# The first state of the later pairs: written by ScalarE instead of by bf16 identity products

## The chip, the cores and the metric

One core of a Trainium2 chip. The metric is the device time of one execution in microseconds (us), lower is better. TensorE (PE) does the products, VectorE (DVE), ScalarE (ACT) and GpSimd (POOL) the rest, and SyncE (SP) starts the DMAs. PSUM has eight banks of 128 partitions x 512 floats.

## The reference, cut to what matters

Two layers over a batch of 8 sequences of 512 tokens, 128 wide. Layer 0 is a random-feature attention, a feed-forward block and an expert block. Layer 1 is a "test-time training" layer and then a mixing block. The part of layer 1 that matters here, for each sequence and each of 16 heads (head size 64), over 8 chunks of 64 tokens:

```python
W, b = W1, b1                       # the same first state for every sequence
for chunk in range(8):
    Z1 = xk @ W + b                 # prediction with the old state
    grad = ...                      # a normalisation and its gradient
    W, b = W - (eta * xk).T @ grad, b - sum(eta * grad)
    Zq = xq @ W + b                 # prediction with the new state
    out = xq + gamma * norm(Zq) + beta
```

Every sequence begins with the same state W1, b1. The kernel holds b1 as the 65th row of W1, so the state of one head is 65 x 64.

## The kernel before, in words

The batch is worked through as four pairs of sequences. Layer 0 of pair p+1 is interleaved by hand with layer 1 of pair p: ORDERS (line 104) has one string per engine, each letter one step. A first string is layer 0 of pair 1 alone, a middle string is used for pairs 1 to 3, a last string is layer 1 of pair 4 alone. Every engine goes through its string in order, so the order on each engine is fixed and only semaphores couple the engines. `0` and `1` are steps of layer 0 for the two sequences, `r` the start of a pair, `s` its first state (two steps, one for each half of 8 heads), `k`, `l` the keys and their transpose, `a` the prediction with the old state, `z`, `b`, `c` the gradient, `d` the update of the state, `q`, `e` the queries and the prediction with the new state, `v`, `w` square roots, `f` and `o` the output, `m` the mixing block. A pair has 16 slots of the letters k to f: 8 chunks x 2 halves of heads.

The running state stays in PSUM: banks 0 and 1 hold the first 8 heads of the two sequences, banks 2 and 3 the other 8 heads. `d` on PE (line 607) adds 32 small products onto them with `start=False`. After each `d` ACT copies two banks (65 x 1024 floats) to w_sb in SBUF (`state`, line 780), which `a` and `e` on PE read (line 546). The semaphore w_ready counts these copies.

The first state of a pair is put into the banks by `start_state` on PE (line 557, products on line 564): three bf16 pieces of the state (w_parts, made by POOL in the setup, lines 1296 and 1298) are multiplied by a bf16 identity and added up, which gives the float value. That is 3 products of 65 x 512 for each of two banks, 6 for a step `s`, 12 for a pair. For pairs 2 to 4 PE first waits for w_ready (ACT's last copy out of the banks). The last product raises w_started. ACT waits for it and makes its usual copy to w_sb.

The order around the start of pairs 2 and 3 is, from the middle string:

```python
"PE":  r k s k l s 1 a 0 0 q 1 l b 0 ...
"ACT": r 0 k s k l 1 s m a 0 v 1 q l ...
"DVE": r 0 m 1 0 1 m a z b c a 0 ...
```

and for pair 4, from the last string, `r k s k l s a b b l q a` on PE and `r m k s l a v k s l a v` on ACT.

Other lines that the steps name: L574, the 16 narrow products of `r` (columns of 16) for the learning rate, on DVE L1133 takes them; L590 `k`, L808 its copy on ACT; L539 `l`, L787 and L788 its two copies on ACT (keys); L815 the square after `a` on ACT, L1099 its sum on DVE; L848 the square root of the mixing block's normalisation on ACT, L1151 and L1153 the DVE steps that use it; L1316 the first step of the gradient on POOL. The setup on POOL (lines 1230 to 1303) counts its steps in pool_set; other engines wait for the total N_POOL_SET before layer 1.

Of the kernel before, what the change touches and what calls it, by code (L numbers as in the profile page):

```python
# [1 line left out]

# [8 lines left out]
ACT = mybir.ActivationFunctionType  # L27
# [3 lines left out]
PAIRS = B // 2  # L31
# [8 lines left out]
H, HD, K = 16, 64, 64  # L40
# [3 lines left out]
HH = H // 2  # L44
HALF = HH * HD
C = HD + 1
# [30 lines left out]
def shape_constants():  # L77
# [21 lines left out]
SLOTS = 2 * NJ  # L99
# [2 lines left out]


ORDERS = {
    "PE": (("011011100011000111011011001010110010110100100010"),
        ("rkskls1a00q1lb0nakqn0kbld1aedl1eabk1bqd0lkfqfaed0lqea1kbqlob0d1fk0eafqbnodnlk111ae1fb1kq1dl0aed10lbfk0aed0qbo0"
          "lfk0q1aedb1lqfkaedo0qbl0fma0kbfd0elokqeam10kl0dfqb0ealq10bd1n01faemdob1qf1dfee01offmo1m"),
        ("rksklsabblqakbldkqaekldbqammedlqkfaefbldokamqedblfkaeqbldmafkbledqkofaelbdqmfakqdebqloakkblfdefalobqdkbaeldqfk"
          "eaqlkdfbeamoqldfebqfaeoqdfbmfemodefmfmommmmm")),
    "ACT": (("110110010100110100111101010100010111100100001010"),  # L110
        ("r0kskl1sna0v1ql0a0kvqnkld1aev1lwdeka1wvq0ldfkqafnedlvqawekvqlw1od0fk10eaf1v1qodnlk1wae1vf0kd11lwa0qev0lkdfwa10"
          "veqowdl0fk1aqevd100lfqwkave0qdol0awfvkm0fdel0kowqamve0kl1dfqwe001alv0dq11mfaew0ndvwo1fq1dfewew0off1mom1"),
        ("rmkslavkslavkqldqakevwldkqamvewldkfqaefvdloaqvwkdelmfkewaqvldwmfkamvelqkdwofavledqfakvwdeqlwoaqvkldkffealvwdko"
          "qavelwdqkfeaqvlwdfkmeaolvwfdeqqwfaewovqfdfemowdmefwmfmommmmm")),
    "DVE": (("110110010100101010111101010100010111100010110000"),
        ("r0n101nazbca0z0bc1aezy1beaczy1bc0a0nze1yaebczy0b1aczb101ecyaez111b1cy0az01e0bcyaz0be01c0ayzbcena0zybcmaey0z10m"
          "0ebca0zye101b0yam1czbc0e011eayzbyc0m1eeyny11m"),
        ("rmmazbaczbcazeybcazeybcazebcamyzebcmayzebcayzebcayzebcamzyebcayzbcazebcyazebcyazemybceamyzebcaeyyzbceymmeymmmm"
          "mm")),
    "POOL": ((""),  # L120
        ("zzzzyyzyzyzooyzyzyzyzzoyoyzozyzyyzyyyooo"),
        ("zzzyzyzyzyzyzoyzzyyzozoyzoyzyyzoyyzyyooo")),
}
BANKS = ("01234567023541670237023541670416273501462735014627350146273501462735014627530146275346754675465764756454756475"
          "76745675475647567467467457456745764564576746746576476456746574657465465475645647654765476574657465746574765745"
# [14 lines left out]

def turns(engine):

    first, middle, last = ORDERS[engine]
    taken = dict.fromkeys(PER_TOKEN, 0)
    for what in first + middle.replace("n", "") + (PAIRS - 2) * middle.replace("n", "m") + last:
        pair, step = divmod(taken[what], PER_TOKEN[what])
        taken[what] += 1
        if pair < PAIRS:
            yield what, pair, step
    assert all(n in (0, PAIRS * PER_TOKEN[what]) for what, n in taken.items()), taken  # L150


# [9 lines left out]
def build(nc, a, out):  # L162
    with ExitStack() as ctx:
        def sb(name, shape, dtype=F32):
            return ctx.enter_context(nc.sbuf_tensor(name, shape, dtype))

        def new_sem(name):
            return ctx.enter_context(nc.semaphore(name))


        ps = ctx.enter_context(nc.psum_tensor("ps", [128, 8, 512], F32))
# [5 lines left out]
        def part(pack, name):  # L177
            at, width = views(PACKS[pack])[0][name]
            return tile[pack][:, at:at + width]
# [8 lines left out]
        w_ga, w_i, lora_b, first = (part("expert", n) for n in ("gate_a", "wi", "lora_b", "first"))  # L188
# [14 lines left out]
        ones_bf = sb("ones_bf", [2 * 32 + 1, 128], BF16)  # L203

        w_parts = sb("w_parts", [C, 3, H, HD], BF16)
        ident_bf = sb("ident_bf", [128, 128], BF16)

        mod_all = sb("mod_all", [128, 12, B])
# [31 lines left out]
        w_sb = w_sb_t[0:C]  # L240
# [36 lines left out]
        s_w0 = k_sc[0:C, :, 0:HD]  # L277
# [12 lines left out]
        S = {n: new_sem(n) for n in names}  # L290
# [3 lines left out]
        pool_set, dve_set, act_set, pe_set = (new_sem(n) for n in ("pool_set", "dve_set", "act_set", "pe_set"))  # L294
# [15 lines left out]
        def loaded(eng, name):  # L310

            eng.wait_ge(loaded_sem[name], 16 * len(loads[name]))

        LEVELS = HD.bit_length() - 1
        N_LAYER0_SET = 6
        N_POOL_SET = N_LAYER0_SET + 4 * 4 + 4 + 1 + 1 + 2 * (4 + 1 + 4) + 1 + 4 + LEVELS + LEVELS + 1 + 4 + 5 * 4 + 4 + 8

        x_dram = a["x"].rearrange("b t p d -> b p t d")
        out_dram = out.rearrange("b (j t) d -> b t j d", t=K)
# [15 lines left out]
        def _(pe):  # L335
            count = [0] * 8
            mm = nc.tensor.matmul
# [16 lines left out]
            def end(ins, b):  # L354
                ins.then_inc(S[f"filled_{b}"], 1)
# [9 lines left out]
            for n in range(12):  # L365
                last = mm(bank[7][:, n * B:(n + 1) * B], s_wmod[:, n * D:(n + 1) * D], s_sig[:, n // 6, :], start=True, stop=True)
# [187 lines left out]
                              start=True, stop=True)  # L554
                end(last, b)

            def start_state(p, f):
                for n in (2 * f, 2 * f + 1):
                    if p:
                        pe.wait_ge(S["w_ready"], (SLOTS + 2) * p - 1 + f)  # L560
                    elif count[n]:
                        pe.wait_ge(S[f"drained_{n}"], count[n])
                    for part in range(3):
                        last = mm(bank[n][0:C, :], ident_bf[0:C, 0:C],
                                  w_parts[:, part, HH * f:HH * (f + 1), :].rearrange("c h d -> c (h d)"),
                                  start=(part == 0), stop=(part == 2), skip_group_check=True)
                last.then_inc(S["w_started"], 1)
# [66 lines left out]
            def mixing(p, step):  # L634
# [18 lines left out]
                elif step == MIX_OUT:  # L653
# [3 lines left out]
                        last = mm(bank[b][:, t * D:(t + 1) * D], kact[:, t * 128:(t + 1) * 128], w_vf[:, :], start=True, stop=True)  # L657
                    end(last, b)

            for what, p, step in turns("PE"):  # L660
                if what in "01":
                    layer0(p, step, int(what))
                elif what == "r":
                    if p == 0:
                        loaded(pe, "ttt")
                        pe.wait_ge(pool_set, N_POOL_SET)
                    start(p)
                elif what == "s":
                    start_state(p, step)
                elif what == "o":  # L670
                    attended(p, step)
                elif what == "m":
                    mixing(p, step)
                else:
                    slot(what, p, step)
# [18 lines left out]
        def _(act):  # L694
            loaded(act, "mod")
            nc.scalar.activation(s_sig[:, :, :], cT, ACT.Sigmoid).then_inc(act_set, 1)
            def root(name, src, dst, u=None, scale=1.0, eps=LN_EPS):

                key = name if u is None else f"{name}_{u}"
                nc.scalar.activation(dst, src, ACT.Sqrt, bias=eps, scale=scale).then_inc(S[key], 1)  # L700
# [13 lines left out]
            def layer0(p, step, u):  # L714
# [51 lines left out]
                elif step == LN5:  # L766
                    if p == 0:
                        act.wait_ge(pool_set, N_POOL_SET)
                    elif p >= 2:
# [4 lines left out]
                if step in roots and (p or step != LN1_STATS):  # L774
                    name = roots[step]
                    act.wait_ge(S[f"{name}_var_{u}"], p + 1)
                    root(f"{name}_std", l["mv"][:, :, 1], l["std"][:, :], u)

            def state(f):
                nc.scalar.copy(w_sb[:, f, :, :, :].rearrange("p b h d -> p (b h d)"),  # L780
                               ps[0:C, 2 * f:2 * f + 2, :].rearrange("p a c -> p (a c)")).then_inc(S["w_ready"], 1)
# [84 lines left out]
            for what, p, step in turns("ACT"):  # L866
                if what in "01":
                    layer0(p, step, int(what))
                elif what == "r":
                    start(p)  # L870
                elif what == "s":
                    act.wait_ge(S["w_started"], 2 * p + step + 1)
                    state(step)
                elif what == "o":
                    attended(p, step)
                elif what == "m":
                    mixing(p, step)
                else:
                    slot(what, p, step)
# [3 lines left out]
        def _(dve):  # L883
# [245 lines left out]
            def start(p):  # L1129
                if p == 0:  # L1130
                    dve.wait_ge(pool_set, N_POOL_SET)
                src = filled(dve, f"rate_{p}")[:, 0:NJ * H].rearrange("p (j h) -> p j h", j=NJ)
# [101 lines left out]
        def _(pool):  # L1234
            P = nc.gpsimd
# [18 lines left out]
            def then_all(instructions):  # L1254

                for ins in instructions:
                    done[0] += 1
                    ins.then_inc(pool_set, 1)
                pool.wait_ge(pool_set, done[0])
# [32 lines left out]
            then(P.tensor_scalar(s_mean[:, :], s_mean[:, :], 1.0 / HD, None, ALU.mult))  # L1292
            heads4 = [slice(4 * n, 4 * n + 4) for n in range(4)]
            then_all(tt(s_w0[:, n, :], s_w0[:, n, :], s_mean[:, n].unsqueeze(2).broadcast_to([C, 4, HD]), ALU.subtract) for n in heads4)
            for part in range(3):
                then_all(P.tensor_copy(w_parts[:, part, n, :], s_w0[:, n, :]) for n in heads4)
                if part < 2:
                    then_all(tt(s_w0[:, n, :], s_w0[:, n, :], w_parts[:, part, n, :], ALU.subtract) for n in heads4)
# [3 lines left out]
            then_all(P.memset(t[HD:C, 4 * n:4 * n + 4, :], 1.0) for t in (kT1, qT1) for n in range(4))  # L1302
            assert done[0] == N_POOL_SET, done
            def heads(ap):
# [84 lines left out]
```

## Time and profile before

| | |
|---|---|
| time, median of 3 runs | 1005.95 us (1004.88 to 1006.24) |
| profiled execution, span from first to last instruction | 1004.5 us |
| profiled execution, own time besides the span | not recorded; the span is 1.45 us under the median |
| PE busy, weight loads busy | 94%, 71% of the span |
| DVE, ACT, POOL busy | 78%, 65%, 34% |
| mean granted TensorE clock | 0.977 of full |

Times in rows are in us from the start of the span, durations in us unless "ns" stands there. L12 is line 12 of the kernel before. PE is the row of products, PEld the loads of the stationary operand. In a granted clock 1.00 is 2.4 GHz and 0.50 is 1.2 GHz; a stretch between these was partly at each.

### The profile page before, as it was taken

How to read it: one execution, taken by the hardware profiler on the slowest of the kernel's cores; microseconds unless marked ns; L12 is line 12 of the kernel's file. 1: busy time of each engine (PE TensorE's matmuls, PEld its weight loads, DVE VectorE, ACT ScalarE, POOL GpSimd, SP SyncE). 2: the span in 40 equal slices, each digit the busy share in tenths (PEclk: the TensorE clock that was granted, in tenths of full speed). 3: DMA queues.
4: the chain of work that ended last, by engine and by line, in shares of the span. 5: the costliest groups of instructions: out<-in, count | busy, mean ns of one | idle time of the engine just before them, and what ended most of it. 6: DMA issues, size and time to landing. Idle time of an engine off the chain costs nothing.

```text
span 1004.5 us, 26971 instructions
## 1 busy us (share of the span) xinstructions
PE 949.1 (94%) x10906; PEld 714.9 (71%) x10906; DVE 787.3 (78%) x1945; ACT 651.5 (65%) x1240; POOL 343.0 (34%) x456
## 2 busy tenths in 40 slices
PE   7788899999999999999999999899999998999995
PEld 5565575778787766787887776677787775777773
DVE  5856359988799679968888769987889847888973
ACT  2642274897856575888666566689765556686762
POOL 1992011343341321333242222143341323454450
PEclk9799999999999999979999989999999989999998
DMA  9000010000000010000000010000000000000000
GB/s 333 14 1 1 11 33 1 2 2 2 3 1 3 22 32 1 3 1 3 2 13 1 12 43 2 2 2 2 2 12 2 12 23 2 2 2 13 2 2 21
DMA packets 15831, 16.14 MB, mean 16 GB/s; under 512 B 2013, under 2 KB 14301, under 8 KB 15325
## 3 DMA queue, kind: packets, MB, share of 16 engines
q1 hardware_dynamic: 15709, 14.43, 4.7%
q8 instruction: 87, 1.43, 0.6%
q14 instruction: 35, 0.29, 0.1%
HBM read 10.23 MB, written 2.10 MB: 12 GB/s over the span
## 4 chain that ended last, share of the span: by engine, by line
PE 62%; DVE 24%; ACT 6%; issue 4%; POOL 3%; DMA 0%; DVEq 0%; ACTq 0%; POOLq 0%; SPq 0%
PE ps L546 8%; PE ps L607 4%; PE ps L539 4%; PE ps L631 4%; PE ps L590 3%; PE ps L601 3%; PE ps L528 3%; PE ps L490 3%; PE ps L613 3%; PE ps L520 3%; PE ps L521 3%; PE ps L499 2%; POOL gbase L1316 2%; DVE kmax L1004 2%; DVE tmp L1110 2%
## 5 line engine op out<-in xcount | busy, mean ns | idle before, releaser
L1316 POOL TENSOR_TENSOR gbase<-zhat,gamma 128x512 f32<-128x512 f32 x64 | 81.2, 1269 | 395.1 <-DVE scl L1104 388.5
L1324 POOL TENSOR_TENSOR zq_sqq<-zq_sqq,qinv 128x512 f32<-128x512 f32 x64 | 68.1, 1069 | 185.1 <-DVE qinv L1127 185.1
L780 ACT COPY w_sb<-ps 65x1024 f32<-65x1024 f32 x72 | 72.6, 1008 | 15.6 <-PE ps L607 12.1
L546 PEld LDWEIGHTS ps<-w_sb,keys 65*64 65x64 f32 x2048 | 66.0, 139 | 18.6 <-issue 10.9
L546 PE MATMUL ps<-w_sb,keys 65*64 65x64 f32 x2048 | 73.8, 226 | 3.8 <-ACT zT L835 1.5
L607 PE MATMUL ps<-grad,k_sc 64*65 64x64 f32 x2048 | 74.4, 222 | 2.6 <-DVE grad L1121 2.3
L607 PEld LDWEIGHTS ps<-grad,k_sc 64*65 64x65 f32 x2048 | 66.0, 135 | 14.8 <-issue 12.5
L1107 DVE TENSOR_TENSOR gbase<-gbase,ps 128x512 f32<-128x512 f32 x64 | 43.6, 681 | 40.7 <-POOL gbase L1316 29.3
L546 PEld LDWEIGHTS ps<-w_sb,queries 65*64 65x64 f32 x2048 | 66.2, 140 | 11.5 <-issue 5.4
L613 PEld LDWEIGHTS ps<-h,pack_ttt 128*128 128x128 f32 x512 | 64.5, 194 | 12.8 <-issue 6.6
L546 PE MATMUL ps<-w_sb,queries 65*64 65x64 f32 x2048 | 73.1, 226 | 0.3 <-ACT queries L788 0.2
L590 PE MATMUL ps<-pack_ttt,h 128*128 128x512 f32 x128 | 71.0, 639 | 0.2
L613 PE MATMUL ps<-h,pack_ttt 128*128 128x128 f32 x512 | 69.4, 279 | 1.3 <-ACT keys L788 0.7
L1319 POOL TENSOR_TENSOR k_sc<-k_tok,scl 128x512 f32<-128x512 f32 x64 | 67.8, 1059 | 0.0
L760 ACT ACTIVATE feats<-ps,pack_cols 128x512 f32<-128x512 f32 x64 | 42.9, 687 | 35.3 <-PE ps L521 28.8
L601 PE MATMUL ps<-w_t,h 128*128 128x512 f32 x128 | 65.4, 592 | 0.0
L808 ACT COPY k_tok<-ps 128x512 f32<-128x512 f32 x64 | 37.4, 585 | 42.9 <-PE ps L590 32.7
L631 PE MATMUL ps<-g_wo,zT 128*128 128x128 f32 x512 | 62.4, 275 | 0.0
L631 PEld LDWEIGHTS ps<-g_wo,zT 128*128 128x128 f32 x512 | 59.7, 192 | 0.0
L1099 DVE TENSOR_REDUCE ssum<-sq 128x8 f32<-128x512 f32 x64 | 42.8, 669 | 15.6 <-ACT sq L815 15.6
L815 ACT ACTIVATE sq<-ps 128x512 f32<-128x512 f32 x64 | 38.4, 599 | 22.7 <-PE ps L546 22.1
L1110 DVE TENSOR_TENSOR tmp<-gbase,zhat 128x512 f32<-128x512 f32 x64 | 49.2, 768 | 2.2
(247 smaller groups left out, 2370.9 us busy)
## 6 DMA issues: line engine op xcount, KB each, us to landing
x<-in_x SPq DMA_DIRECT2D x8, 256.0 KB, 3.4
xc<-x SPq DMA_DIRECT2D x16, 128.0 KB, 2.4
out_x<-xc SPq DMA_DIRECT2D x16, 128.0 KB, 2.4
pack_ttt<-in_ttt SPq DMA_DIRECT2D x1, 1216.0 KB
keys<-in_gam_bet_rows SPq DMA_DIRECT2D x1, 1024.0 KB
w_sb<-in_compose SPq DMA_DIRECT2D x1, 1024.0 KB, 10.5
pack_expert<-in_expert SPq DMA_DIRECT2D x1, 792.0 KB, 16.8
zq_sqq<-in_wmod SPq DMA_DIRECT2D x1, 768.0 KB, 4.5
```

Of the source, the lines that this page charges most:

```text
L546: last = mm(bank[b][64 * c:64 * c + 64, (h % HH) * HD:(h % HH + 1) * HD], src[:, h, 64 * c:64 * c + 64], w_sb[:, f, c, h % HH, :], start=T ...
L590: end(mm(bank[b], chunk(p, j), w_k1[:, cols], start=True, stop=True), b)
L601: end(mm(bank[b], chunk(p, j), w_t1[:, cols], start=False, stop=True), b)
L607: last = mm(bank[2 * f + c][0:C, h * HD:(h + 1) * HD], k_sc[64 * c:64 * c + 64, HH * f + h, :], grad[64 * c:64 * c + 64, h, :], start=Fals ...
L613: last = mm(bank[b][:, n * 128:(n + 1) * 128], w_q1[:, (4 * f + n) * 128:(4 * f + n + 1) * 128], chunk(p, j), start=True, stop=True)
L631: last = mm(bank[b][:, 0:D], zT[:, g, :], g_wo[:, g, :], start=False, stop=(g == HP - 1))
L780: nc.scalar.copy(w_sb[:, f, :, :, :].rearrange("p b h d -> p (b h d)"), ps[0:C, 2 * f:2 * f + 2, :].rearrange("p a c -> p (a c)")).then_in ...
L1107: V.tensor_tensor(gbase[:, cols], gbase[:, cols], filled(dve, f"t1_{g}"), ALU.add).then_inc(drained(f"t1_{g}"), 1)
L1110: half_way[0] = go_on(V.tensor_tensor(tmp[:, :], gbase[:, cols], zhat[:, cols], ALU.mult))
L1316: P.tensor_tensor(gbase[:, cols], zhat[:, cols], gamma2[:, cols], ALU.mult).then_inc(S["g_hat"], 1)
L1319: P.tensor_tensor(k_sc[:, hs, 0:HD], heads(k_tok[:, cols]), per_head(scl[:, hs]), ALU.mult)
L1324: P.tensor_tensor(heads(zq_hat[:, cols]), heads(zq_hat[:, cols]), per_head(qinv[:, hs]), ALU.mult).then_inc(S["zq_ready"], 1)
```

## The change

For pair 1 nothing changes. For pairs 2 to 4 the step `s` does nothing on PE. On ACT it waits until the last update of those banks in the pair before is done, and then writes twice from w_first, a float copy of the first state that POOL makes in the setup with four more copies: into the two PSUM banks, and into w_sb. The orders are written out for all four pairs, with the same letters in the same places on every engine. The wait for the end of the setup on PE stands before the first letter of layer 1, which is `r` of pair 1 as before.

```diff
 def turns(engine):
-    first, middle, last = ORDERS[engine]
     taken = dict.fromkeys(PER_TOKEN, 0)
-    for what in first + middle.replace("n", "") + (PAIRS - 2) * middle.replace("n", "m") + last:
+    for what in ORDERS[engine]:
         pair, step = divmod(taken[what], PER_TOKEN[what])
         taken[what] += 1
-        if pair < PAIRS:
-            yield what, pair, step
+        yield what, pair, step
...
         w_parts = sb("w_parts", [C, 3, H, HD], BF16)
+        w_first = sb("w_first", [C, 2, HH, HD])
...
-        N_POOL_SET = N_LAYER0_SET + ... + 1 + 4 + 5 * 4 + 4 + 8
+        N_POOL_SET = N_LAYER0_SET + ... + 1 + 4 + 4 + 5 * 4 + 4 + 8
...
-            def start_state(p, f):
+            def start_state(f):
                 for n in (2 * f, 2 * f + 1):
-                    if p:
-                        pe.wait_ge(S["w_ready"], (SLOTS + 2) * p - 1 + f)
-                    elif count[n]:
+                    if count[n]:
                         pe.wait_ge(S[f"drained_{n}"], count[n])
                     for part in range(3):
                         last = mm(...)
...
                 elif what == "s":
-                    start_state(p, step)
+                    if p == 0:
+                        start_state(step)
...
+            def state0(f):
+                first = w_first[:, f, :, :].rearrange("p h d -> p (h d)").unsqueeze(1).broadcast_to([C, 2, HALF])
+                nc.scalar.copy(ps[0:C, 2 * f:2 * f + 2, :], first)
+                nc.scalar.copy(w_sb[:, f, :, :, :].rearrange("p b h d -> p b (h d)"), first).then_inc(S["w_ready"], 1)
+
...
                 elif what == "s":
-                    act.wait_ge(S["w_started"], 2 * p + step + 1)
-                    state(step)
+                    if p == 0:
+                        act.wait_ge(S["w_started"], step + 1)
+                        state(step)
+                    else:
+                        act.wait_ge(S["dw_done"], SLOTS * p - 1 + step)
+                        state0(step)
...
             then_all(tt(s_w0[:, n, :], s_w0[:, n, :], s_mean[:, n].unsqueeze(2).broadcast_to([C, 4, HD]), ALU.subtract) for n in heads4)
+            then_all(P.tensor_copy(w_first[:, n // 2, 4 * (n % 2):4 * (n % 2) + 4, :], s_w0[:, heads4[n], :]) for n in range(4))
             for part in range(3):
```

## Rows read from the trace of the kernel before

**Rows 1.** The page: the chain that ended last, by engine.
```profile
PE 62%; DVE 24%; ACT 6%; issue 4%; POOL 3%; DMA 0%; DVEq 0%; ACTq 0%; POOLq 0%; SPq 0%
```

**Rows 2.** Groups (mean ns): ACT's state copy; L564: min/median/max ns, first and last start.
```profile
L780 ACT COPY w_sb<-ps 65x1024 f32<-65x1024 f32 x72 | 72.6, 1008 | 15.6 <-PE ps L607 12.1 <-PE ps L564 2.8
...
L564 PE MATMUL ps<-w_parts,ident_bf x48: 377/380/634, 134.3 to 827.9; 65*65 65x512 bf16 x48
```

**Rows 3.** The longest wait of PE between 364 and 590 us (us, times, longest).
```profile
PE ps L412 <- ACT ek L730: 1.5, 2, 0.7
```

**Rows 4.** Timeline, start of pair 2 (start, us, engine, line).
```profile
357.11 1.46 PE L564 MATMUL ps<-w_parts,ident_bf 65*65 65x512 bf16 x6
...
358.51 0.57 ACT L808 COPY k_tok<-ps 128x512 f32<-128x512 f32 x1
358.97 1.01 ACT L780 COPY w_sb<-ps 65x1024 f32<-65x1024 f32 x1
...
359.88 0.59 ACT L808 COPY k_tok<-ps 128x512 f32<-128x512 f32 x1
...
360.95 0.58 ACT L788 COPY keys<-ps 64x512 f32<-64x512 f32 x1
...
361.66 1.01 ACT L780 COPY w_sb<-ps 65x1024 f32<-65x1024 f32 x1
361.68 1.15 PE L546 MATMUL ps<-w_sb,keys 65*64 65x64 f32 x32 [0.51 <-ACT keys L788]
...
362.57 0.20 ACT L848 ACTIVATE std<-mv 128x4 f32<-128x4 f32 x1
...
363.28 1.11 DVE L1153 TENSOR_SCALAR hat<-xc,mv,inv 128x128 f32<-128x128 f32 x4
```

**Rows 5.** Timeline, start of pair 3.
```profile
585.89 1.93 PE L574 MATMUL ps<-w_theta,h 128*128 128x16 f32 x16
...
589.50 2.77 PE L564 MATMUL ps<-w_parts,ident_bf 65*65 65x512 bf16 x6
...
590.42 0.57 ACT L808 COPY k_tok<-ps 128x512 f32<-128x512 f32 x1
...
592.31 1.01 ACT L780 COPY w_sb<-ps 65x1024 f32<-65x1024 f32 x1 [1.32 <-PE ps L564]
...
596.44 1.15 PE L546 MATMUL ps<-w_sb,keys 65*64 65x64 f32 x32
...
597.46 0.20 ACT L848 ACTIVATE std<-mv 128x4 f32<-128x4 f32 x1
...
597.90 1.12 DVE L1153 TENSOR_SCALAR hat<-xc,mv,inv 128x128 f32<-128x128 f32 x4
```

**Rows 6.** Timeline, start of pair 4.
```profile
822.23 0.57 ACT L808 COPY k_tok<-ps 128x512 f32<-128x512 f32 x1
...
823.83 1.01 ACT L780 COPY w_sb<-ps 65x1024 f32<-65x1024 f32 x1 [1.03 <-PE ps L564]
...
828.25 1.15 PE L546 MATMUL ps<-w_sb,keys 65*64 65x64 f32 x32
...
831.38 1.01 ACT L780 COPY w_sb<-ps 65x1024 f32<-65x1024 f32 x1
```

**Rows 7.** Windows: length, busy time of PE, PEld, DVE, ACT, POOL, then granted clock, DMA.
```profile
356.10:366.33 10.23, 9.72 (x82) 6.43 (x79) 9.23 (x46) 8.77 (x17) 0.00 (x0) 1.00 0.11 28
588.01:600.97 12.96, 12.96 (x82) 7.80 (x79) 9.42 (x46) 9.05 (x17) 0.00 (x1) 0.74 0.08 21
426.46:444.96 18.50, 18.50 (x192) 15.50 (x192) 12.81 (x24) 14.50 (x26) 6.20 (x7) 0.72 0.00 1
661.11:676.76 15.65, 15.38 (x192) 12.45 (x192) 12.29 (x23) 14.22 (x26) 5.67 (x7) 0.89 0.01 3
```

**Rows 8.** Timeline of POOL: its setup.
```profile
72.74 1.42 POOL L1296 CAST w_parts<-k_sc 65x256 bf16<-65x256 f32 x4
...
78.53 1.92 POOL L1302 MEMSET queries<- 1x512 f32 x4
```

More of the change, by code:

```diff
@@ L104 @@
 ORDERS = {
[L105 to L122, printed above, removed]
+    "PE": ("011011100011000111011011001010110010110100100010rkskls1a00q1lb0akq0kbld1aedl1eabk1bqd0lkfqfaed0lqea1kbqlob0d1fk0eafqbodlk111ae1fb1kq1dl0aed10lbfk0aed0qbo0lfk0q1aedb1lqfkaedo0qbl0fma0kbfd0elokqeam10kl0dfqb0ealq10bd101faemdob1qf1dfee01offmo1mrkskls1a00q1lb0makqm0kbld1aedl1eabk1bqd0lkfqfaed0lqea1kbqlob0d1fk0eafqbmodmlk111ae1fb1kq1dl0aed10lbfk0aed0qbo0lfk0q1aedb1lqfkaedo0qbl0fma0kbfd0elokqeam10kl0dfqb0ealq10bd1m01faemdob1qf1dfee01offmo1mrkskls1a00q1lb0makqm0kbld1aedl1eabk1bqd0lkfqfaed0lqea1kbqlob0d1fk0eafqbmodmlk111ae1fb1kq1dl0aed10lbfk0aed0qbo0lfk0q1aedb1lqfkaedo0qbl0fma0kbfd0elokqeam10kl0dfqb0ealq10bd1m01faemdob1qf1dfee01offmo1mrksklsabblqakbldkqaekldbqammedlqkfaefbldokamqedblfkaeqbldmafkbledqkofaelbdqmfakqdebqloakkblfdefalobqdkbaeldqfkeaqlkdfbeamoqldfebqfaeoqdfbmfemodefmfmommmmm"),
@@ new lines @@
+    "ACT": ("110110010100110100111101010100010111100100001010r0kskl1sa0v1ql0a0kvqkld1aev1lwdeka1wvq0ldfkqafedlvqawekvqlw1od0fk10eaf1v1qodlk1wae1vf0kd11lwa0qev0lkdfwa10veqowdl0fk1aqevd100lfqwkave0qdol0awfvkm0fdel0kowqamve0kl1dfqwe001alv0dq11mfaew0dvwo1fq1dfewew0off1mom1r0kskl1sma0v1ql0a0kvqmkld1aev1lwdeka1wvq0ldfkqafmedlvqawekvqlw1od0fk10eaf1v1qodmlk1wae1vf0kd11lwa0qev0lkdfwa10veqowdl0fk1aqevd100lfqwkave0qdol0awfvkm0fdel0kowqamve0kl1dfqwe001alv0dq11mfaew0mdvwo1fq1dfewew0off1mom1r0kskl1sma0v1ql0a0kvqmkld1aev1lwdeka1wvq0ldfkqafmedlvqawekvqlw1od0fk10eaf1v1qodmlk1wae1vf0kd11lwa0qev0lkdfwa10veqowdl0fk1aqevd100lfqwkave0qdol0awfvkm0fdel0kowqamve0kl1dfqwe001alv0dq11mfaew0mdvwo1fq1dfewew0off1mom1rmkslavkslavkqldqakevwldkqamvewldkfqaefvdloaqvwkdelmfkewaqvldwmfkamvelqkdwofavledqfakvwdeqlwoaqvkldkffealvwdkoqavelwdqkfeaqvlwdfkmeaolvwfdeqqwfaewovqfdfemowdmefwmfmommmmm"),
@@ new lines @@
+    "DVE": ("110110010100101010111101010100010111100010110000r0101azbca0z0bc1aezy1beaczy1bc0a0ze1yaebczy0b1aczb101ecyaez111b1cy0az01e0bcyaz0be01c0ayzbcea0zybcmaey0z10m0ebca0zye101b0yam1czbc0e011eayzbyc0m1eeyy11mr0m101mazbca0z0bc1aezy1beaczy1bc0a0mze1yaebczy0b1aczb101ecyaez111b1cy0az01e0bcyaz0be01c0ayzbcema0zybcmaey0z10m0ebca0zye101b0yam1czbc0e011eayzbyc0m1eeymy11mr0m101mazbca0z0bc1aezy1beaczy1bc0a0mze1yaebczy0b1aczb101ecyaez111b1cy0az01e0bcyaz0be01c0ayzbcema0zybcmaey0z10m0ebca0zye101b0yam1czbc0e011eayzbyc0m1eeymy11mrmmazbaczbcazeybcazeybcazebcamyzebcmayzebcayzebcayzebcamzyebcayzbcazebcyazebcyazemybceamyzebcaeyyzbceymmeymmmmmm"),
@@ L123 @@
+    "POOL": ("zzzzyyzyzyzooyzyzyzyzzoyoyzozyzyyzyyyooozzzzyyzyzyzooyzyzyzyzzoyoyzozyzyyzyyyooozzzzyyzyzyzooyzyzyzyzzoyoyzozyzyyzyyyooozzzyzyzyzyzyzoyzzyyzozoyzoyzyyzoyyzyyooo"),
 }
@@ L315, in build @@
         N_LAYER0_SET = 6
-        N_POOL_SET = N_LAYER0_SET + 4 * 4 + 4 + 1 + 1 + 2 * (4 + 1 + 4) + 1 + 4 + LEVELS + LEVELS + 1 + 4 + 5 * 4 + 4 + 8
+        N_POOL_SET = N_LAYER0_SET + 4 * 4 + 4 + 1 + 1 + 2 * (4 + 1 + 4) + 1 + 4 + LEVELS + LEVELS + 1 + 4 + 4 + 5 * 4 + 4 + 8
         x_dram = a["x"].rearrange("b t p d -> b p t d")
@@ L658, in mixing @@
                     end(last, b)
+            layer1_set = False
             for what, p, step in turns("PE"):
@@ L662, in _ @@
                     layer0(p, step, int(what))
[L663 to L666, printed above, removed]
+                    continue
+                if not layer1_set:
+                    loaded(pe, "ttt")
+                    pe.wait_ge(pool_set, N_POOL_SET)
+                    layer1_set = True
+                if what == "r":
                     start(p)
                 elif what == "s":
-                    start_state(p, step)
+                    if p == 0:
+                        start_state(step)
                 elif what == "o":
```

## The prediction

> **What bounds the kernel now.** I read the chain of waits first, since it says which engine sets the end: PE has 62% of it, DVE 24%, ACT 6% [rows 1]. The waits of PE say how much room there is between the starts of pairs: from 364 to 590 us its longest group of waits is 1.5 us in all [rows 3]. So inside a pair the kernel runs at the pace of PE's order, and what PE loses or wins at the start of a pair stays in the time. Then the timeline of the three starts that the change touches, [rows 4 to 6]. They differ, and that decides the case. At the start of pair 2, ACT does not wait for the identity products: the key copy begins at 358.51 and the state copy follows at 358.97, as fast as ACT can. PE's prediction at 361.68 waits 0.51 us for ACT's key copy (L788 at 360.95) [rows 4]. The 12 products lie inside time in which PE would have waited anyway. At the starts of pairs 3 and 4, ACT waits 1.32 and 1.03 us for the products [rows 5, 6]: there PE is late. The windows say why: the same stretch, from the learning-rate sum on DVE to the first gradient step on POOL, with the same 82 products, takes 10.23 us at a granted clock of 1.00 and 12.96 us at 0.74 [rows 7], a stretch that was partly at 1.2 GHz. Six products took 1.46 us at full clock and 2.77 us at half [rows 4, 5].
>
> **What the change removes.** 36 of the 48 products of L564 [rows 2], 12 for each of pairs 2 to 4. If PE's time counted in full, 12 of them are worth 2.9 us at full clock (two groups of 1.46) and up to 5.5 us at half (two of 2.77) [rows 4, 5]. It also removes PE's wait for w_ready and ACT's wait for w_started. ACT's new wait for dw_done is for an update that lies before the whole output and mixing work of the last pair, so I count it as zero. PE's prediction still waits for w_ready, and it comes behind the key copies that stand behind the state copies on ACT.
>
> **What it adds on ACT.** Each of six steps makes two copies of 65 x 1024 instead of one. ACT's copy PSUM to SBUF takes 1.008 us [rows 2], and the next instruction starts 0.91 us after it (358.97 to 359.88) [rows 4]. No row shows ACT writing to PSUM. From below, the columns alone: (1.01 - 0.57) / 512 = 0.86 ns for a column, 0.88 us for 1024 [rows 4]. From above, 1.1 us, the whole row and a little for an operand that this trace does not show. I take 0.91, the spacing of the same shape: 5.5 us of ACT for six steps. The Trainium skill (ScalarE: Activation LUTs, "ACT is a hardware spline evaluator") says that ScalarE reaches PSUM faster than SBUF; no row here shows it, and by it the added copy would be at the lower end, 0.03 us less for each.
>
> **Start of pair 2.** Up to 358.97 nothing moves. PE's prediction waits for the key copies, which stand behind one state step: +0.91 us. The square root L848 stands behind both state steps on ACT: 362.57 + 1.82 = 364.39. Its DVE step L1153 follows it by 0.44 us where it waits for it (597.46 to 597.90) [rows 5], so it starts at 364.83 instead of 363.28: +1.55 us [rows 4]. On DVE it stands ahead of the sum L1099 that leads to the gradient, so the first gradient step comes 1.55 us later. PE waits for the results of that chain some microseconds on. I take **+1.55 us** for this start; the ends are +0.9 (only PE's own delay counts) and +1.8 (both copies count in full).
>
> **Start of pair 3.** The order is the same as for pair 2, and the products no longer hold ACT. So at full clock the stretch would take 10.23 + 1.55 = 11.78 us instead of 12.96: **-1.18 us** [rows 7]. By the other way: key copy 590.42, state step at 590.88 without the wait, two copies to 592.70, then the same 1.80 us from key copy to prediction as in pair 2 (359.88 to 361.68), so the prediction is at 594.50 instead of 596.44, and L848 at 592.70 + 2.69 + 0.91 = 596.30 instead of 597.46, -1.16 [rows 4, 5]. Both agree, the DVE chain being what comes last.
>
> **Start of pair 4.** The last string has the state step right before the key copies. Key copy 822.23, state step 822.69 instead of 823.83, two copies to 824.51, then key copies 0.59 apart and 0.73 us from the second to the prediction (360.95 to 361.68): 825.83 instead of 828.25, -2.42 us. The second state step comes 2.42 us earlier (828.96 instead of 831.38) but has one more copy, 0.91, ahead of the keys of slot 1: **-1.5 us** for what follows [rows 6]. In this pair the chain goes through ACT and DVE, so I take this smaller figure.
>
> **Elsewhere.** POOL's four more copies of 65 x 256 cost some 1.4 us (four casts of this shape took 1.42), and POOL's setup ends at 80.5 us while the first state is made at 134.3 [rows 8, 2]: hidden, by some 50 us. If that cover were gone it would be the 1.4 us.
>
> **The clock.** Sum so far: 1.55 - 1.18 - 1.5 = -1.1 us. This supposes full clock after the change. But the change leaves PE without work between the second key transpose and the prediction: the 1.46 us of six products, plus 0.91 us, at the place where PE now waits 0.51, about 2.9 us at the start of pair 2. The clock fell in the stretch of 12.96 us without any such gap, after 16 products of 16 columns (1.93 us for them) [rows 5], so PE is near that edge at each start. What a low stretch costs here is bounded by the 2.73 us between the two windows [rows 7]; 1.31 us of it is the first six removed products (2.77 - 1.46), which leaves at most 1.4 us. DVE's chain covers part of that. I take 0.5 us for each of three starts, +1.5, so the sum is between -1.1 and +0.4. I take the middle, -0.3: 1004.5 becomes 1004.2 as a span, and against the median 1005.95, which is 1.45 above the span, **1005.6 us**.
>
> **A second effect of the clock.** Inside pairs 2 and 3 the same 192 products take 18.50 us at 0.72 and 15.65 us at 0.89 [rows 7]. Nothing in the order differs. The change moves the later one or the earlier one by a microsecond or two against the chip's clock decisions, so 2.85 us can go either way.
>
> **Rivals.**
> (A) Forecast: ACT's second copy takes the place of the products; the first start loses, the other two win, net near zero. Chance 0.52, own range 1004.1 to 1007.9.
> (B) Faster by clock: the low stretch inside pair 2 shortens to that of pair 3, and the starts cost nothing more: -1.1 - 2.85 = -4 us, 1002.0; with only half of it about 1003.3. For it: the before kernel had the long form once. Against: nothing in the change aims at it. Chance 0.19.
> (C) Faster by PE: the products' time comes off in full, because ACT runs ahead. Two groups of 1.46 at pair 2, and 2.77 + 1.46 or more at each other start: 2.9 + 4.2 + 4.2 = 11 us, 994.6. Against it: at the start of pair 2 PE already waits for ACT [rows 4]. Chance 0.06.
> (D) Slower by clock: with nothing to do at each start, PE falls to 1.2 GHz there and starts the dense work behind it (transposes, queries, layer 0) at half rate. That happens in this kernel already (0.74) [rows 7]. Price: the full 1.4 us at each start instead of 0.5, -1.1 + 4.2 = +3.1, 1009.0, and with a long stretch in pair 3 too up to 1011.9. It decides from the point where a start keeps more than 1 us of low clock behind the prediction. Chance 0.23. The Trainium skill (TensorE: Matmul & The Clock Gate, "Why this matters for your kernels") warns that idle gaps between bursts of products put the engine back to half clock; by that rule the change, which turns products into a gap, ends here. The trace agrees only in part: the clock fell at the start of pair 3 while PE was busy with narrow products.
> (E) The change does not do what it says, as ACT's write into PSUM could not begin before some other release. By the code dw_done is long reached. It would show as a wait ahead of the new copy; small, within (A).
>
> **How the numbers follow.** About 0.2% (2.0 us) is what a measurement of this kernel can tell from no change. Faster: B and C, 0.25. Same: A, with its range nearly inside the bound, 0.52. Slower: D, 0.23. The range runs from 1002.0 (B in full) to 1009.4 (D with every start, just beyond 1009.0); C and D with the long stretch are left out, some 0.15.
>
> **What would show it.** Right: six new ACT copies into PSUM of 0.9 to 1.1 us with no wait ahead of them; 12 products of L564 left; at pair 2 the prediction 0.9 us later than 361.68 with PE waiting some 3 us for ACT's key copies; L848 at 364.4; the stretch from learning-rate sum to first gradient step near 11.8 us at both starts; pair 4 shorter by 1.5 us. Wrong: if that stretch is under 10.5 us at pair 2 (C), if it is over 13 us with a low clock behind the prediction (D), if the copy into PSUM takes much over 1.1 us, or if POOL's setup shows up as a wait in layer 1. The granted clock inside pairs 2 and 3 tells B from the rest.

## The result, and the profile after

The changed kernel takes 1007.99 us (median of 20 runs, 1003.67 to 1011.89). The kernel before, in 20 runs, takes 1002.98 (995.91 to 1008.15). The ratio is 1.0053, 95% interval 1.0032 to 1.0073: slower by half a percent. Both kernels scatter far more than the three runs of before suggested: those three lay 1.9 to 3.3 us above the median of twenty. In the experiments before was run another 109 times, with a mean of 1002.67 us (standard error 0.34), and the changed kernel has 32 runs in all, with 1007.65 (0.36). The difference of 4.98 us is what has to be explained. The number in brackets behind a mean is its standard error. (Left out everywhere are four disturbed executions of 1357 to 3242 us, two of before and two of experiments, and one slow run of an experiment, 1019.52 us at a clock of 0.927, while one run of before that counts as slow only just, 1010.11 us, is kept: without it the mean is 1002.60.)

The page of the changed kernel: busy times, the chain by engine, and the groups of the prediction's products and of ACT's copy out of PSUM. Lines are those of the changed kernel; L515 was L546, L756 was L780, L764 was L788.

```profile
PE 945.9 (94%) x10870; PEld 716.3 (71%) x10870; DVE 786.9 (78%) x1945; ACT 657.2 (65%) x1246; POOL 343.1 (34%) x460
...
PE 64%; DVE 23%; ACT 5%; issue 4%; POOL 3%; DMA 0%; DVEq 0%; ACTq 0%; POOLq 0%; SPq 0%
...
L515 PE MATMUL ps<-w_sb,keys 65*64 65x64 f32 x2048 | 75.1, 228 | 10.8 <-ACT keys L764 8.3
...
L756 ACT COPY w_sb<-ps 65x1024 f32<-65x1024 f32 x66 | 66.5, 1008 | 12.9 <-PE ps L574 12.2
```

36 products are gone and six ACT copies came. PE's busy time fell by 3 us only (949.1 before), and PE now waits 8.3 us for ACT's key copies ahead of the prediction. The new copies by line (min/median/max ns, first and last start), with no wait ahead of them:

```profile
L752 ACT COPY ps<-w_first x6: 1005/1012/1015, 367.3 to 834.3; 65x1024 f32<-65x1024 f32 x6
L753 ACT COPY w_sb<-w_first x6: 1038/1042/1046, 368.3 to 835.3; 65x1024 f32<-65x1024 f32 x6
```

The timeline at the start of pair 2, to be read against [rows 4]:

```profile
366.85 0.57 ACT L784 COPY k_tok<-ps 128x512 f32<-128x512 f32 x1
367.31 1.01 ACT L752 COPY ps<-w_first 65x1024 f32<-65x1024 f32 x1
...
367.56 0.63 PE L508 MATMUL ps<-pack_attn,k_tok 128*128 128x128 f32 x4 [1.09 <-ACT k_tok L784]
...
368.26 1.04 ACT L753 COPY w_sb<-w_first 65x1024 f32<-65x1024 f32 x1
...
369.21 0.58 ACT L784 COPY k_tok<-ps 128x512 f32<-128x512 f32 x1
...
370.28 0.58 ACT L764 COPY keys<-ps 64x512 f32<-64x512 f32 x1
...
371.00 1.51 PE L515 MATMUL ps<-w_sb,keys 65*64 65x64 f32 x32 [2.81 <-ACT keys L764]
```

A state step on ACT takes 1.90 us (367.31 to 369.21) where it took 0.91 (358.97 to 359.88) [rows 4]. PE has nothing to do for 1.09 and then for 2.81 us, where it waited 0.51 before. And the prediction itself runs slowly in part, 1.51 us instead of 1.15: the clock has fallen.

For the rest I use one measure: the **start** of a pair, from the learning-rate sum on DVE to the first gradient step of the third slot on POOL. Windows over these starts for pairs 2, 3 and 4 (columns as in [rows 7]), before:

```profile
356.10:390.40 34.30, 33.31 (x325) 22.50 (x322) 30.79 (x92) 25.24 (x49) 5.28 (x6) 1.00 0.04 9
588.01:625.05 37.04, 36.59 (x325) 23.92 (x322) 30.99 (x92) 25.52 (x49) 5.29 (x6) 0.91 0.03 8
819.83:848.14 28.31, 25.54 (x260) 15.60 (x257) 17.36 (x43) 15.86 (x29) 5.76 (x7) 0.88 0.04 11
```

and of the changed kernel:

```profile
364.44:400.79 36.35, 32.39 (x313) 22.77 (x310) 30.87 (x92) 27.32 (x51) 4.82 (x6) 0.95 0.03 8
594.05:631.88 37.83, 33.91 (x313) 23.76 (x310) 30.87 (x92) 27.32 (x51) 4.82 (x6) 0.91 0.03 9
825.14:852.62 27.48, 22.83 (x248) 14.14 (x245) 17.45 (x43) 17.72 (x31) 5.74 (x6) 0.88 0.05 11
```

ACT is 2 us busier in each start. The three starts together differ by 2.0 us only (101.66 against 99.65). The rest of the 4.5 us between these two profiles lies where PE, DVE and ACT have the same instructions: up to the start of pair 2 the changed kernel had lost 8.3 us (364.44 against 356.10), and from the end of each of the first two windows to the next start it took 4.35 us less (193.26 against 197.61) and 1.52 us less (193.26 against 194.78), because half-clock stretches fell there or not. So two profiles can't settle this case; the experiments had to.

The prediction was written for a shorter stretch, from the learning-rate sum to the first gradient step. Of the changed kernel for pairs 2, 3 and 4, and then of before for pair 4:

```profile
364.44:376.25 11.81, 7.91 (x64) 5.89 (x61) 9.41 (x46) 10.10 (x18) 0.00 (x0) 0.86 0.10 24
594.05:605.87 11.82, 7.98 (x60) 6.27 (x57) 9.41 (x46) 9.53 (x17) 0.00 (x1) 0.76 0.10 24
825.14:835.08 9.94, 8.08 (x49) 4.14 (x46) 4.77 (x20) 7.29 (x13) 0.00 (x0) 0.69 0.11 28
...
819.83:832.11 12.28, 12.28 (x67) 6.30 (x63) 4.76 (x20) 6.50 (x12) 0.00 (x0) 0.72 0.09 23
```

### The profile page after: what moved, and what is told of

The parts are those of the page before. It is cut to its first block, busy times and chain, and to the rows that moved or that the text cites. A ratio compares the mean times of both kernels' runs of the same rounds, so it can differ in the third digit from the quotient of the medians.

```text
span 1009.0 us, 26909 instructions
## 1 busy us (share of the span) xinstructions
PE 945.9 (94%) x10870; PEld 716.3 (71%) x10870; DVE 786.9 (78%) x1945; ACT 657.2 (65%) x1246; POOL 343.1 (34%) x460
## 3 DMA queue, kind: packets, MB, share of 16 engines
HBM read 10.23 MB, written 2.10 MB: 12 GB/s over the span
## 4 chain that ended last, share of the span: by engine, by line
PE 64%; DVE 23%; ACT 5%; issue 4%; POOL 3%; DMA 0%; DVEq 0%; ACTq 0%; POOLq 0%; SPq 0%
PE ps L515 8%; PE ps L598 4%; PE ps L574 4%; PE ps L508 4%; PE ps L568 4%; PE ps L580 3%; PE ps L497 3%; PE ps L459 3%; PE ps L557 3%; PE ps L490 3%; PE ps L489 3%; PE ps L468 2%; DVE kmax L984 2%; POOL gbase L1297 2%; PE ps L421 2%
## 5 line engine op out<-in xcount | busy, mean ns | idle before, releaser
L515 PE MATMUL ps<-w_sb,keys 65*64 65x64 f32 x2048 | 75.1, 228 | 10.8 <-ACT keys L764 8.3
L515 PEld LDWEIGHTS ps<-w_sb,keys 65*64 65x64 f32 x2048 | 67.1, 141 | 24.9 <-issue 17.2
L756 ACT COPY w_sb<-ps 65x1024 f32<-65x1024 f32 x66 | 66.5, 1008 | 12.9 <-PE ps L574 12.2
L515 PEld LDWEIGHTS ps<-w_sb,queries 65*64 65x64 f32 x2048 | 65.7, 139 | 10.8 <-issue 3.9
L515 PE MATMUL ps<-w_sb,queries 65*64 65x64 f32 x2048 | 72.6, 225 | 0.3 <-ACT queries L764 0.2
L557 PE MATMUL ps<-pack_ttt,h 128*128 128x512 f32 x128 | 68.7, 624 | 0.2
```

Of the source, the lines that this page charges most:

```text
L515: last = mm(bank[b][64 * c:64 * c + 64, (h % HH) * HD:(h % HH + 1) * HD], src[:, h, 64 * c:64 * c + 64], w_sb[:, f, c, h % HH, :], start=T ...
L557: end(mm(bank[b], chunk(p, j), w_k1[:, cols], start=True, stop=True), b)
```

## The experiments

"Before" in this section is the mean of its 109 runs, 1002.67. Each run lists its span and its mean granted clock. From them I take the time at half clock as 2 x (1 - clock) x span. Over the 109 runs of before a line fits: 0.40 us of span for each us at half clock. The experiments test three theories: 1, the change costs time only by a lower clock; 2, the added ACT copies cost time by themselves; 3, added on the way, the forecast rested on a profile whose starts 3 and 4 were at half clock.

**Before, again.** No edit.

> The kernel before, run again for its own clocks and a second profile. Theory 1 (the change costs time at half clock only): a run of before with the same mean granted clock as a run of the changed kernel has the same span within 1 us, for instance 1004.5 us at 0.977 and 1006.5 at 0.975, and the mean clock of before over the runs is about 0.006 higher than the 0.976 of the changed kernel. Rival 2 (the ACT copies cost time by themselves): at equal clock before is 4 to 5 us shorter, and the mean clocks are equal.

Measured: mean 1001.13 of 12 runs, median 1002.15; 35 runs of the same kernel taken beside them gave 1003.83 as a median, and the interval of the ratio (0.993 to 0.999) leaves out 1. A kernel differs from itself here by 0.4%, so one comparison of twelve runs against thirty-five can't carry a verdict at this size, and I pool. The second profile repeats the first: start 3 takes 37.04 us at a clock of 0.91, start 4 28.32 at 0.88. By the line, before has a span of 1001.8 us at 40 us of half clock and the changed kernel 1002.4; before spends 37.7 us at half clock on average (mean clock 0.981), the changed kernel 47.8 (0.976). Of 109 runs of before 38 have a clock of 0.983 or more; of 32 of the changed kernel none. This looked like theory 1, the clock alone. The next runs showed that it is not: at half clock PE, not ACT, sets part of the starts, and hides the price.

**Unused products in the gap.** PE gets full-array bf16 products ahead of the prediction:

```diff
 WARM = {
+    "z_16": 12, "z_32": 12, "z_48": 7,
```

> The changed kernel with unused full-array bf16 products (128x512) in the gap that PE has at each of the three starts: 12 ahead of the prediction of pairs 2 and 3, 7 ahead of that of pair 4 (12 x 0.213 us = 2.6 us in a gap of 2.8). Theory 1: no half-clock stretch begins behind the start of pairs 2 to 4, the dense products behind it run at full rate, each start gets 0.5 to 1.4 us shorter, the median falls by 2 to 5 us against the changed kernel (1008.0) to 1003 to 1006. Rival 2: no change beyond 1 us, as PE's products were not what is waited for.

Measured: mean 1004.53 (0.68), 3.1 us under the changed kernel and 1.9 above before. Its clock is 0.985, above before's. Windows of its starts:

```profile
360.08:396.00 35.92, 33.77 (x325) 22.28 (x322) 31.01 (x92) 27.04 (x51) 5.29 (x7) 1.00 0.04 9
589.31:625.23 35.92, 33.82 (x325) 22.27 (x322) 31.00 (x92) 27.03 (x51) 5.29 (x7) 1.00 0.04 9
818.53:845.47 26.94, 21.34 (x255) 13.48 (x252) 17.46 (x43) 17.64 (x31) 5.75 (x6) 1.00 0.05 12
```

All three are at full clock, so the gap does lower the clock and filling it holds it. But they are 35.92 us, not 34.30: a cost that no clock explains. Three of its runs, at a mean clock of 0.987, took 1003.50 us; twelve runs of before at 0.987 took 998.24, 5.3 us less. Three runs are few: all twelve have a mean span of 1002.4 us at 30.6 us of half clock, where the line of before gives 998.0, so with the 0.33 us outside the span (below) it is 4.7. At the same high clock the change costs 4.7 to 5.3 us. Theory 2 had forecast no change beyond 1 us from these products, and theory 1 no cost at full clock: each misses one half of it.

**All four copies ahead of the start.** In ACT's string `ss` stands ahead of `r` for pairs 2 to 4:

```diff
-... m1r0kskl1sm ... m1rmkslavkslav
+... m1ssr0kkl1m ... m1ssrmklavklav
```

> The changed kernel with ACT's two state steps ahead of the start of the pair in ACT's order, where ACT waited 2.5 us for the learning-rate sum; the four copies take 3.7 us. Rival 2 (ACT's second copies on the path are the price): PE's prediction comes 2 to 2.5 us earlier, the gap of 2.8 us nearly closes, and the median falls by 5 to 7 us against the changed kernel (three starts), to 1001 to 1003. Theory 1: the starts get shorter by the same path, and the low clock behind them goes too, as the gap closes; so it is the profile's clock behind the starts that must be high as well. If it stays low with the gap closed, theory 1 falls.

Measured: mean 1006.56 (0.60) of 11 runs, 1.1 us under the changed kernel, which is no clear gain. The copies end too late for the place they were put in (timeline of ACT and the learning-rate sum at pair 2):

```profile
357.92 1.01 ACT L752 COPY ps<-w_first 65x1024 f32<-65x1024 f32 x1
...
360.30 0.28 DVE L1113 TENSOR_TENSOR eta<-ps,pack_rows 128x128 f32<-128x128 f32 x1
...
360.75 1.05 ACT L753 COPY w_sb<-w_first 65x1024 f32<-65x1024 f32 x1
361.70 0.31 ACT L768 ACTIVATE eta<-eta 128x128 f32<-128x128 f32 x1
...
364.51 0.63 PE L508 MATMUL ps<-pack_attn,k_tok 128*128 128x128 f32 x4 [2.18 <-ACT k_tok L784]
```

The sum starts at 360.30 and its sigmoid on ACT at 361.70, 1.40 us later, where it was 0.31 in the changed kernel (364.44 to 364.75); the first key copy behind it moves back with it. The expected 5 to 7 us were wrong: I had counted the room of 2.5 us and put 3.7 us into it. PE's gap moved ahead of the key transposes (2.18 us), with 1.35 us more ahead of the prediction, and the clock stayed low, 0.978. It says nothing on the price of one copy.

**The removed products back, unused.** Six products of the removed shape at each place where six were taken, into a bank that PE owns anyway:

```diff
+                for _ in range(6 if name in ("k1_17", "z_16", "k1_33", "z_32", "k1_49", "z_48") else 0):
+                    mm(bank[b][0:C, :], ident_bf[0:C, 0:C], w_parts[:, 0, 0:HH, :].rearrange("c h d -> c (h d)"), start=True, stop=True)
```

> The changed kernel with six unused products of the removed shape (65x65 by 65x512, bf16) at each place where six were removed, into a bank that PE owns anyway. PE has its old work, ACT its new. Theory 1 in the form that any work in the gap keeps the clock: the low stretches become those of the kernel before, median within 1.5 us of before plus 1.5 (three starts, ACT part alone). Theory 1 in the form that these narrow products count for little: clock as in the changed kernel (0.976 mean), median 1008 or up to 3 us more, since a start at half clock pays 2.77 us for six. Rival 2: same as the changed kernel within 1 us.

Measured: mean 1006.56 (0.60), median 1007.55, clock 0.982. With PE's old work and ACT's new work the kernel keeps nearly the clock of before (0.981) and is still 3.9 us slower. Two of its starts were at full clock, 35.94 and 26.95 us, as with the full-array products; start 2 was at 0.95, 36.39 us. PE waits for ACT all the same, here at start 2:

```profile
363.23 1.46 PE L319 MATMUL ps<-w_parts,ident_bf 65*65 65x512 bf16 x6
366.19 1.25 PE L517 MATMUL ps<-w_sb,keys 65*64 65x64 f32 x32 [1.50 <-ACT keys L766]
```

So the larger part comes with ACT's new work. A third theory had to be added before the next runs: the starts of pairs 3 and 4, which seemed to win, had been compared with starts of before at half clock.

**Before, with products that hold its clock.** Four at each start:

```diff
 WARM = {
+    "k1_16": 4, "k1_32": 4, "k1_48": 4,
```

> The kernel before with four unused full-array bf16 products (0.85 us) behind the narrow products of each of the three starts, to see all three starts of before at full clock. Theory 3 (the profile that the forecast rested on had two of three starts at half clock by luck, and at full clock the change costs at every start): start 3 (learning-rate sum to the gradient step two slots on) takes 34.3 plus at most 0.85 us instead of 37.05, start 4 some 26 plus 0.85 instead of 28.3, so that the changed kernel's 35.92 and 26.94 at full clock are losses of 1.6 and about 0.5 to 1. Theory 1 alone (only clock): start 4 of before at full clock is not shorter than 26.9 minus its dummies.

Measured: mean 1001.43 (0.77), clock 0.985. Its starts, all at full clock:

```profile
359.36:394.01 34.65, 34.01 (x329) 22.95 (x326) 30.90 (x92) 25.37 (x49) 5.29 (x6) 1.00 0.04 9
587.27:621.98 34.71, 34.07 (x329) 22.96 (x326) 30.89 (x92) 25.37 (x49) 5.29 (x7) 1.00 0.04 9
816.76:842.59 25.83, 23.01 (x264) 14.60 (x261) 17.36 (x43) 15.87 (x29) 5.75 (x7) 1.00 0.05 12
```

The four products cost 0.35 us at pair 2 (34.65 against 34.30). Start 3 of before is 34.7 at full clock with them, some 34.4 without, and not 37.04; start 4 is 25.8, some 25.5 without the products, and not 28.3. Against these the changed kernel's 35.92, 35.92 and 26.94 (its gap filled) lose 1.6, 1.6 and 1.1 to 1.5 us. The third theory holds, in that the two starts were measured at half clock. That this was chance is not shown: start 3 was at 0.91 in both profiles of before, both of executions with a mean clock of 0.977, below the 0.981 of all runs.

**One copy moved.** The two copies into PSUM go into ACT's wait for the learning-rate sum; w_sb is written where it was:

```diff
+                elif what == "t":          # "tt" ahead of "r"
+                    if p:
+                        act.wait_ge(S["dw_done"], SLOTS * p - 1 + step)
+                        nc.scalar.copy(ps[0:C, 2 * step:2 * step + 2, :], first_of(step))
 def state0(f):
-                nc.scalar.copy(ps[0:C, 2 * f:2 * f + 2, :], first)
```

> The changed kernel with the two copies into PSUM moved ahead of the start of the pair on ACT, into its 2.5 us wait for the learning-rate sum; the copies to w_sb stay where they are, one for each state step as in before. If ACT's second copy is the price of 1.6 us, start 2 takes 34.3 to 34.6 us at full clock instead of 35.92, and PE's gap ahead of the prediction shrinks from 2.8 to about 2 us. The low clock behind the starts then is somewhat rarer, median 1003 to 1006, 2 to 4 us under the changed kernel. If the price is not ACT's second copy, start 2 stays at 35.9.

Measured: mean 1003.22 (0.53), 4.4 us under the changed kernel and level with before. Its starts:

```profile
362.11:397.60 35.49, 32.47 (x313) 22.68 (x310) 30.69 (x92) 25.43 (x49) 4.83 (x7) 0.95 0.04 9
590.89:626.39 35.50, 32.53 (x313) 22.76 (x310) 30.69 (x92) 25.45 (x49) 4.83 (x6) 0.95 0.04 9
819.68:846.23 26.55, 21.34 (x248) 13.44 (x245) 17.45 (x43) 15.84 (x29) 5.75 (x6) 0.94 0.05 12
```

The expected 34.3 to 34.6 us at full clock did not show, as each start held a half-clock stretch behind the gap, which was still 1.87 us. But the stretch to the first gradient step at pair 2 is 10.24 us (362.11 to 372.35), that of before (10.23) and not the 11.81 of the changed kernel.

**One copy moved, and the gap filled.** The same with `"z_16": 7, "z_32": 7, "z_48": 3` unused products, run twice.

> As e6_split, with 7, 7 and 3 unused full-array products in what is left of the gap (1.5 us of 2). Both prices gone: starts at 34.3 to 34.6 us and no low stretch behind them; against e6_split the median falls by 1 to 3 us, to 1001 to 1003, level with before or up to 2 us under it.

> The version with the copies into PSUM moved ahead of the start and unused products in the gap, again, for more runs: mean 1001.3 with 12 runs so far against 1002.8 of before. If it beats before, the ratio is again under 1 (0.997 to 0.999); if that was chance, 1.000.

Measured: the starts in the first of the two profiles, all at full clock:

```profile
360.35:394.65 34.30, 32.37 (x319) 21.84 (x317) 30.80 (x92) 25.23 (x49) 5.29 (x6) 1.00 0.04 9
587.94:622.26 34.32, 32.44 (x320) 21.84 (x317) 30.80 (x92) 25.24 (x49) 5.29 (x6) 1.00 0.04 10
815.54:840.57 25.03, 20.48 (x251) 13.09 (x248) 17.39 (x43) 15.74 (x29) 5.75 (x7) 1.00 0.05 12
```

35.92 against 34.30 is the price of the copy into PSUM at its old place, 1.62 us at pairs 2 and 3, and 1.9 at pair 4 (26.94 against 25.03). The means are 1001.28 (0.56) and 1000.75 (0.46), 1001.01 (0.36) together in 24 runs. Ratios to before are 0.9987 (0.9963 to 1.0012) and 0.9990 (0.9964 to 1.0016). Pooled over all runs the gain on before is 1.66 us with a standard error of 0.50: probably real, 0.17%, but each comparison by itself includes no change, and the pooled error leaves out the 0.4% by which before differed from itself above.

**The changed kernel, again.**

> The changed kernel again, for a second profile and for more runs on this chip. Median 1007 to 1009, mean clock 0.976, no run above 0.983; a half-clock stretch within 5 us behind the prediction of each of pairs 2 to 4 if the gap causes it, in whatever place the clock's decisions fall.

Measured: mean 1007.58 (0.54), clock 0.976; none of the twelve had a clock above 0.980. The starts, each with a half-clock stretch behind the gap, as in the first profile:

```profile
357.28:393.66 36.38, 32.42 (x313) 22.83 (x310) 30.87 (x92) 27.23 (x51) 4.82 (x6) 0.95 0.03 9
586.92:624.93 38.01, 34.10 (x313) 23.80 (x310) 30.88 (x92) 27.34 (x51) 4.82 (x6) 0.91 0.04 9
818.19:845.68 27.49, 22.84 (x248) 13.96 (x245) 17.45 (x43) 17.73 (x31) 5.75 (x7) 0.88 0.05 11
```

**POOL's part alone.** Before with w_first and its four copies, which nothing reads.

> The kernel before with POOL's four more copies alone (nothing reads them). All theories: no effect inside the span, same line of span against low clock as before (1001.8 us at 40 us of half clock, within 0.4), mean time within noise of 1002.8. If the 0.33 us that the changed kernel takes more outside its span comes from the new tile or the copies, it shows here (2.13 instead of 1.80 between time and span); if it comes from ACT's copies or the missing products, it stays at 1.80.

Measured: mean 1002.22 (1.32) of 11 runs, 1002.0 at 40 us of half clock: nothing inside the span. But between time and span it has 2.12 us, as has every kernel with w_first (2.10 to 2.14), while before has 1.80. So 0.33 us of the slowdown lies outside the span and comes with this tile or its copies. Which of the two, and why, was not tried. No trace of it is read here.

**ACT's half alone.** PE keeps its 36 products; ACT writes w_sb from w_first and no longer waits for them:

```diff
-                    act.wait_ge(S["w_started"], 2 * p + step + 1)
-                    state(step)
+                        first = w_first[:, step, :, :].rearrange("p h d -> p (h d)").unsqueeze(1).broadcast_to([C, 2, HALF])
+                        nc.scalar.copy(w_sb[:, step, :, :, :].rearrange("p b h d -> p b (h d)"), first).then_inc(S["w_ready"], 1)
```

> Half of the change: PE still writes the banks with its 36 products, ACT writes w_sb from the float copy without waiting for them, one copy a step. If ACT's second copy (the one into PSUM) is the price at full clock, start 2 is 34.3 us at full clock as in before, not 35.92. If the gap in PE's work is what lowers the clock, the clock is that of before (mean 0.981, some runs at 0.985 and above) and not 0.976. Median 1001 to 1004, within 2 us of before. If instead the cost lies in ACT reading w_first or in the order of waits, it is 1006 or more.

Measured: mean 1002.43 (1.02) of 11 runs, clock 0.982 as before. Its starts:

```profile
362.09:396.41 34.32, 33.28 (x325) 22.51 (x322) 30.82 (x92) 25.23 (x49) 5.29 (x7) 1.00 0.04 9
594.04:630.85 36.81, 36.60 (x325) 23.87 (x322) 30.91 (x92) 25.54 (x49) 5.30 (x7) 0.91 0.03 8
824.14:849.23 25.09, 22.24 (x260) 14.20 (x257) 17.40 (x43) 15.78 (x29) 5.75 (x7) 1.00 0.05 12
```

Start 2 is 34.32 us at full clock. So neither ACT reading w_first nor the freed wait costs anything that shows; it takes the second copy to lose the 1.6 us. Start 4, at full clock and with PE's products in place, is 25.09, so the loss of the changed kernel's 26.94 there may be up to 1.9 us.

The four versions of the change side by side (mean us, mean clock; the cell with both is 24 runs, that with neither 32):

| | gap left | gap filled |
|---|---|---|
| copy into PSUM in the state step | 1007.65, 0.976 | 1004.53, 0.985 |
| copy into PSUM ahead of the start | 1003.22, 0.979 | 1001.01, 0.982 |

Moving the copy is worth 4.4 and 3.5 us, filling the gap 3.1 and 2.2. Both act; that the copy weighs more is not clear of the noise (1003.22 against 1004.53, with errors of 0.53 and 0.68). The two are not quite apart either: moving the copy also shortens the gap, from 2.81 to 1.87 us, and the filling is 12, 12 and 7 products in one row and 7, 7 and 3 in the other.

## Why the prediction was wrong

**What bounds the kernel.** Right: PE's order inside a pair keeps what a start loses; the inside of pair 2, from the end of one window to the next start, takes 193.3 us in all nine profiles that have it at full clock. "PE waits for ACT at the start of pair 2" was right and is the core of the case.

**Cost of the copies.** Nearly right. I took 0.91 us for the copy into PSUM; it takes 1.012 us with 0.95 between starts, and the copy from SBUF to SBUF 1.042. The Trainium skill (ScalarE: Activation LUTs, "ACT is a hardware spline evaluator") has ScalarE faster into PSUM than into SBUF, and here the trace agrees, by 0.03 us.

**Start of pair 2.** Right: +1.55 forecast, +1.62 measured at full clock (35.92 against 34.30), through the DVE chain behind L848; to the first gradient step it was 11.81 against 10.23. That it is the copy is shown by the version with the copy moved.

**Starts of pairs 3 and 4.** This is the step that failed. "At full clock the stretch would take 11.78 us instead of 12.96: -1.18" set a start at full clock against one that before had run partly at half clock, and "-1.5" for pair 4 did the same. I had read in the windows that pair 3 was at 0.74, and still took that profile for the kernel. Before at full clock has some 34.4 and 25.1 to 25.5 us there, and the change costs +1.6 and +1.1 to +1.9 instead of -1.18 and -1.5. With the +1.6 of pair 2 and 0.33 outside the span that is 4.6 to 5.4 us, against the measured 4.7 to 5.3 at the same high clock. That it is also near the 4.98 over all runs is partly luck, as there the changed kernel is at half clock more than before.

The length of the stretch itself was forecast well: 11.78 us for pair 3, 11.82 measured, in both profiles, and at pair 4 9.94 instead of 12.28. The gain did not last even against the half-clock start. Up to the third slot, start 3 at the same mean clock of 0.91 took 37.83 and 38.01 us where before had 37.04: its half-clock stretch now lay behind the gap and took back more than the 1.14 us. Only at pair 4 did a part of the forecast gain appear, 27.48 against 28.31 at 0.88.

**The clock.** Right in kind and too small in its weight. All six profiled starts of the changed kernel held a half-clock stretch; of nine profiled starts with the gap filled by full-array products eight were at full clock, and one (25.46 us at 0.93) fell ahead of the gap. The rule of the Trainium skill (TensorE: Matmul & The Clock Gate, "Why this matters for your kernels"), that gaps between bursts cost the clock, is borne out by the filled kernels. I took 0.5 us for each start and 1.4 at most. Against the filled kernel the changed one's starts are longer by 0.4 to 0.5 (36.35 and 36.38 against 35.92), by 1.9 and 2.1 (37.83 and 38.01 against 35.92) and by 0.5 (27.48 and 27.49 against 26.94): 2.9 to 3.1 in all instead of 1.5, start 3 beyond my bound, and filling the gap gives back 3.1 in the mean. Rival D had 4.2 for this and 0.23; its sign, a stretch over 13 us to the first gradient step, did not show. And D put the loss on the clock alone, on top of -1.1; measured are +4.6 to 5.4 from copies and outside the span at full clock, and a lower clock, which before has too in many of its runs (71 of 109 under 0.983). The two do not add up to the 4.98, since before pays for half clock too: with the gap filled the change is 1.9 us above before's mean, and the open gap adds the other 3.1. At half clock before itself waits for the products (ACT 1.32 us at start 3 [rows 5]), so there the change saves something against its copies.

**The level.** I added 1.45 us to a span of 1004.5 and forecast 1005.6 on the basis of three runs around 1006. Twenty runs have 1002.98. So 1007.99 lies inside the stated range by luck, as the forecast was too high for no change and too low in the change: -0.3 us forecast, +5.0 measured. (Time less span is 1.80 us for before, not 1.45.) **Rivals B and C**: C is excluded (PE waits for ACT). B, a shorter half-clock stretch inside pair 2, did happen in both profiles of the changed kernel (none at all there; 193.26 us against 197.61) and was outweighed.

**POOL.** Hidden inside the span, as forecast; the 0.33 us outside it were not foreseen.

## What to carry to other kernels

Before taking work off the busiest engine, look at who is waited for at that very place: here PE had 94% and still waited for ACT where its products went, so a second copy on ACT was dearer than six products. Compare stretches only at equal granted clock; a start that "wins" against one at half clock can be a loss, and one profile and three runs don't show which clock is usual. Put replacement work where the new engine waits (here ahead of the learning-rate sum), but no more than fits: two copies fitted and saved 4.4 us, four did not and saved 1.1 at most, within the noise.

## What the runs showed of the hardware

The same program on one core spreads over 15 us (994.8 to 1010.1 in 109 runs), and the mean granted clock (0.972 to 0.990) orders nearly all of it: 998.24 us at 0.987, 1003.71 at 0.980, 1007.57 at 0.975 (means of 12, 22 and 7 runs). Whether products of 65 x 65 by 512 columns in bf16 hold the clock less well than full-array ones was not settled: with them the clock was 0.982 and with full-array ones 0.985, but half of the former stood at another place, and PE still waited 1.50 us behind them where it waited 0.23 behind the latter. In before, PE stayed at half clock while six of them ran back to back at the start of pair 3 (2.77 us) [rows 5]. ACT copies 65 x 1024 floats in 1.008 us from PSUM to SBUF, in 1.012 from SBUF to PSUM and in 1.042 from SBUF to SBUF.
